# ScalarE copies the first step's columns in two parts, most of them before stage A ends

## The reference, cut to what matters

```python
xf = jnp.fft.rfft2(x, axes=(1, 2), norm='ortho').reshape(B, H, W // 2 + 1, 8, 96)
o1r = relu(xr @ w1[0] - xi @ w1[1] + b1[0])          # per block of 96 channels
o1i = relu(xi @ w1[0] + xr @ w1[1] + b1[1])
o2r = o1r @ w2[0] - o1i @ w2[1] + b2[0]
o2i = o1i @ w2[0] + o1r @ w2[1] + b2[1]
o = softshrink(stack([o2r, o2i]), 0.01)
out = jnp.fft.irfft2(complex(o), s=(H, W), axes=(1, 2), norm='ortho') + x
```

## Time and profile before

| | |
|---|---|
| median of 3 runs | 5809.21 us (5808.68 to 5814.81) |
| the profiled execution, its own time | 5797.72 us |
| its span in the trace | 5795.8 us |
| mean granted clock of TensorE | 0.986 of full |
| busy PE, ACT, DVE, POOL | 96%, 63%, 62%, 22% of the span |

### The profile page before, as it was taken

How to read it: one execution, slowest core, us unless ns; L and a number is a source line. 1 busy time by engine, 2 the same in 40 slices (tenths; PEclk the granted TensorE clock), 3 DMA queues, 4 the chain that set the end, 5 groups by cost and what they waited for, 6 DMA issues and landing times.

```text
span 5795.8 us, 116890 instructions
## 1 busy us (share of the span) xinstructions
PE 5579.8 (96%) x41056; PEld 5526.2 (95%) x41056; DVE 3599.6 (62%) x7158; ACT 3651.7 (63%) x8208; POOL 1264.6 (22%) x810
## 2 busy tenths in 40 slices
PE   8999999999999999999999999999999999999997
PEld 8999999999999999999999999999999999999997
DVE  5656656566566665666756667566665666656666
ACT  6656666566666666656676666665666666567564
POOL 2211222112222022220222202222012221122200
PEclk9999999999999999999999999999999999999999
DMA  3331233312333113332133331233312333113311
GB/s 98 91 92 32 61 92 91 92 34 59 92 91 92 45 47 92 91 92 57 40 88 91 92 80 34 70 91 92 86 36 62 91 92 90 46 48 91 92 45 44
DMA packets 1118349, 426.50 MB, mean 74 GB/s; under 512 B 1117472, under 2 KB 1117600, under 8 KB 1117728
## 3 DMA queue, kind: packets, MB, share of 16 engines
q1 hardware_dynamic: 1117728, 418.29, 28.7%
HBM read 216.89 MB, written 201.33 MB: 72 GB/s over the span
## 4 chain that ended last, share of the span: by engine, by line
PE 94%; issue 2%; DVE 1%; ACT 1%; DMA 0%; DVEq 0%; SPq 0%; ACTq 0%
PE psum L508 16%; PE psum L521 12%; PE psum L522 12%; PE psum L568 12%; PE psum L532 12%; PE psum L552 6%; PE psum L554 6%; PE psum L580 3%; PE psum L549 3%; PE psum L550 3%; PE psum L551 3%; PE psum L581 3%; PE psum L582 3%; DVE x L474 1%; ACT columns L317 0%
## 5 line engine op out<-in xcount | busy, mean ns | idle before, releaser
L293 POOL TENSOR_TENSOR doubled<-x 128x768 f32<-128x768 f32 x248 | 359.8, 1451 | 4206.6 <-DMA x<-x 4186.5
L444 DVE TENSOR_SCALAR relu<-psum,b1t 128x128 f32<-128x128 f32 x1056 | 370.1, 351 | 1364.0 <-ACT hidden_high L359 1361.6
L521 PE MATMUL psum<-w1t,columns 96*128 96x192 f32 x4160 | 1036.7, 331 | 66.7 <-ACT columns L317 66.7
L522 PE MATMUL psum<-w1t,columns 96*128 96x192 f32 x4160 | 1030.0, 330 | 0.0
L508 PEld LDWEIGHTS psum<-mats,x 128*96 128x96 f32 x8192 | 932.4, 168 | 90.0 <-issue 67.9
L508 PE MATMUL psum<-mats,x 128*96 128x128 f32 x8192 | 941.5, 279 | 79.1 <-issue 62.5
L353 ACT ACTIVATE mixed<-psum 128x384 f32<-128x384 f32 (+1 forms) x1056 | 512.8, 486 | 746.7 <-PE psum L522 740.9
L380 ACT ACTIVATE sums_high<-psum 128x512 fp32r<-128x512 f32 x768 | 459.4, 598 | 764.1 <-PE psum L568 764.1
L532 PE MATMUL psum<-mats,mixed 128*128 128x128 f32 x6272 | 874.8, 275 | 0.0
L532 PEld LDWEIGHTS psum<-mats,mixed 128*128 128x128 f32 x6272 | 842.8, 192 | 0.0
L521 PEld LDWEIGHTS psum<-w1t,columns 96*128 96x128 f32 x4160 | 755.4, 199 | 73.6 <-ACT columns L317 73.6
(11 more groups left out here) (62 smaller groups left out, 8421.9 us busy)
## 6 DMA issues: line engine op xcount, KB each, us to landing
x<-x SPq DMA_DIRECT2D x160, 768.0 KB, 7.1
out<-x SPq DMA_DIRECT2D x160, 768.0 KB, 8.2
x<-x SPq DMA_DIRECT2D x32, 1488.0 KB, 10.2
out<-x SPq DMA_DIRECT2D x32, 1488.0 KB, 10.6
x<-x SPq DMA_DIRECT2D x32, 816.0 KB, 5.0
out<-x SPq DMA_DIRECT2D x32, 816.0 KB, 4.5
w2t<-L_conv_w SPq DMA_DIRECT2D x128, 36.0 KB
w2t<-L_conv_w SPq DMA_DIRECT2D x128, 24.0 KB
```

What stands on the lines that cost most here:

```text
L521: pe.matmul(bank_b(s)[:, k], re, w1t[par][:, BLOCK:], start=True, stop=False)
L522: last = pe.matmul(bank_b(s)[:, k], im, w1t[par][:, :2 * BLOCK], start=False, stop=True)
```

## The change

`gather(0)` is taken apart. Stage A runs from both ends to the middle, so after 24 of its 32 groups the slots 0 to 47 and 80 to 127 are in `U`. Behind the eviction of group 24 ACT now waits for `u_zeroed` and for its own count of 24, and copies these 96 slots of column 0 in two instructions (48 slots each); behind the eviction of group 25 it copies those of column 64, in two more. At the end of stage A it copies the middle 32 slots of each column, in two instructions, and the last of these counts `gathered`. The other steps keep their one instruction. No instruction of PE, DVE, POOL or SP changes.

```diff
+EARLY = 24
+INNER = (EARLY // 2 * A_SLOTS, SIZE - EARLY // 2 * A_SLOTS)
 ...
             def gather(s):
                 dst, k = columns[s % 2], len(STEPS[s])
-                if s == 0:
-                    for r, j in enumerate((0, SIZE)):
-                        last = act.activation(dst[:, :, :, r], U[0:BLOCK, :, j:j + 2].rearrange("p s k -> p k s"), ACT.Copy)
-                else:
-                    ...
-                last.then_inc(gathered, 1)
+                j = 2 * STEPS[s][0]
+                act.activation(dst[:, 0:k], U[0:BLOCK, :, j:j + 2 * k].rearrange("p s (k r) -> p k s r", r=2),
+                               ACT.Copy).then_inc(gathered, 1)
+
+            def gather_first(r, lo, hi):
+                j = r * SIZE
+                return act.activation(columns[0][:, :, lo:hi, r], U[0:BLOCK, lo:hi, j:j + 2].rearrange("p s k -> p k s"), ACT.Copy)
 ...
                         last.then_inc(a_copied, 1)
-                    act.wait_ge(u_zeroed, n + 2)
+                        if i + 1 == EARLY:
+                            act.wait_ge(u_zeroed, n + 2)
+                            act.wait_ge(a_copied, n * NA + EARLY)
+                        if i + 1 - EARLY in range(2):
+                            r = i + 1 - EARLY
+                            gather_first(r, 0, INNER[0])
+                            gather_first(r, INNER[1], SIZE)
                     act.wait_ge(a_copied, n * NA + NA)
-                    gather(0)
+                    gather_first(0, *INNER)
+                    gather_first(1, *INNER).then_inc(gathered, 1)
                     gather(1)
```

More of the change, by code:

```diff
@@ L314, in gather @@
                 dst, k = columns[s % 2], len(STEPS[s])
-                if s == 0:
-                    for r, j in enumerate((0, SIZE)):
-                        last = act.activation(dst[:, :, :, r], U[0:BLOCK, :, j:j + 2].rearrange("p s k -> p k s"), ACT.Copy)
-                else:
-                    j = 2 * STEPS[s][0]
-                    last = act.activation(dst[:, 0:k], U[0:BLOCK, :, j:j + 2 * k].rearrange("p s (k r) -> p k s r", r=2),
-                                          ACT.Copy)
-                last.then_inc(gathered, 1)
+                j = 2 * STEPS[s][0]
[4 more added lines that the diff above has]
+                return act.activation(columns[0][:, :, lo:hi, r], U[0:BLOCK, lo:hi, j:j + 2].rearrange("p s k -> p k s"), ACT.Copy)
             with act.Fori(0, PAIRS) as m:
```

## The result

The changed kernel takes 5756.25 us (median of 5 runs, 5752.93 to 5766.13), the kernel before in the same sessions 5811.16 us. The ratio is 0.9905 with a 95% interval from 0.9891 to 0.992: faster by 0.95%, 55 us. The forecast was 5752, with a range from 5737 to 5776. The profiled execution of the changed kernel took 5760.14 us, its span is 5758.2 us.

A forecast was written before the change was run, and what follows sets the result against it. PE, busy 96% of the span, was taken as the bound. A shorter wait before B (23.4 us) and no clock falls behind it (34.3 us) gave 57.7 us off 5809.2, so 5751.5 us, range 5737 to 5776.

The forecast's parts named there:

- The bound and the path: PE, 96% busy, sets the end; the gap before B shrinks 0.73 us a unit, 23.4 us in all.
- The price of the copies: ACT's line 325: 188 ns fixed plus 1.89 per element, so 309 ns for 64 elements, 369 for 96.
- What hides the four early copies: Stage A: ACT's idle 0.28 us before each eviction hides their 1.19 us; lag gone before the last group; cost nothing.
- the earlier wait for `u_zeroed`: ACT waits 8 groups earlier in stage A; 5.8 us of margin in second units; cost nothing.
- The clock: Behind the gap before B: all 14 falls of PE's clock go at 1.35 us, worth 34.3 us.
- rival 2: End copies shorten less: gap 1.76 us, wait worth 10 us, half the clock's share gives 5782 us; chance 0.08.
- What can spread it: Pair starts: four pairs more or fewer at the dearer price, 8 us; stalls from POOL's fold, 1.3 us each.
- the stalls beside POOL: First steps: DVE's subtraction slows beside POOL's fold and PE stands; a few more units at 1.3 us each.
- the dearer stage A: Behind the clock's fall at a pair's start, stage A takes 31.02 us or 29.56; 8 of 15 paid the former.
- Rival 1: Behind the gap before B the clock falls as often as before; only 23.4 us won, 5785.8 us; chance 0.08.
- rival 4: ACT copies cost the same whatever their size; gap 2.24 us, slower at 5819 us; chance 0.03.
- Rival 3: Stalls beside POOL in pairs' first units: 12 more at 1.3 us take back 16 us, 5767 us; chance 0.05.

The follow-up runs named there:

- The long pair at the end: Changed kernel with its four early copies, but the pair at the end of stage A copies all 128 slots again: 5811.1 us, ratio 1.0004.
- the filler in the gap: Kernel before with five matmuls of 128x128, result unread, on PE between stage A and B: 5760.0 us, ratio 0.9914.
- the later POOL: Changed kernel, but POOL starts to fold an input only when DVE is through the running unit's third step: 5754.8 us, ratio 0.9907.
- the two fastest kernels: Changed kernel plus copies by column, more early copies, later fold, filler before E, and three fillers before B (5712.8 us) or before the last step's D (5711.1 us).

## Why the prediction was right

- *The bound and the path.* Right. PE stayed the bound (97% busy), and the whole 0.78 us came through to PE in each unit: gap -25.0 us against -23.4 forecast. The long pair at the end undid it.
- *The price of the copies.* Right: 312 and 371 ns against 309 and 369. The 0.833 ns per element of the Trainium skill (ScalarE: Activation LUTs, What ACT_TABLE_LOAD costs) would have made the copy of 64 elements 239 ns long; the trace has 312, and it decides. The reason that I gave for the 1.89 ns per element, that each is read from another place, was wrong in the main: read as neighbours the copy still took 657 ns of 672, and written side by side 539. The 0.05 us too much was the second wait, which I had left at the end of stage A in the sum, although the change moves it.
- *What hides the four early copies, and the earlier wait for `u_zeroed`.* Right: the lag is gone at the 29th group, and with early copies and a long pair the time was that of the kernel before (ratio 1.0004, 0.9993 to 1.0014).
- *The clock.* Right in the main: 14 falls before, none after, and the filler in the gap shows that this term does not need the shorter wait. But my reason was only that 1.35 us is next to gaps that never had a fall, and nothing I had told where between 1.26 and 2.08 us the falls begin; that 1.30 us was short enough was in part luck. At 1.78 us 10 falls of 14 are left, where rival 2 had given back half of the clock's share for 1.76. The price of 34.3 us also holds one stall of 1.26 us (in the stretch of 105.70) that is none of the clock's.
- *What can spread it.* Named, and it came on the bad side: the stalls beside POOL took some 6 us (8 units, where I had "a few more"; 5.9 us is what the later POOL gave back), three more pairs paid the dearer stage A, and the standstill at the pairs' starts was 4.4 us longer. My reason for more stalls, that the fallen clock hides them, is not borne out: the kernels with 10 to 16 falls and a gap of 1.78 to 2.02 us have 5 to 8 of them. The stretches miss their forecast by 8.4 us in all; what the other 2.5 are is open. The falls before stage E, 5.9 us in the profile, I had not foreseen: none of these gaps had a fall in the trace that I read. This is why the stretches and stages behind the gap gave 20.0 us in the profile and not 34.3.
- *The rivals.* Rival 1 is refuted by the profile after (no fall) and rivals 2 and 4 by the durations of the copies. Rival 3 holds as a part, with some 6 us in place of 16.

In the medians the sum was 57.7 forecast and 54.9 measured. In the profiled pair it was 57.7 and 37.6 (5740.0 us forecast for the profiled execution, 5760.1 measured; sum of the stretches 3280 and 3289.7, mean clock 0.991 and 0.989). So the close fit of the medians is in part luck: the profiled pair fell 20.1 us short of the sum by the losses above, and the medians lie 17.3 us further apart than the pair, whose execution of the kernel before was a fast one.

## What to carry to other kernels

Ask of every gap of the bounding engine not only how long it is but what clock stands behind it; here the stretches behind the gaps were worth as much as the gaps themselves (25.9 and 25.0 us), and a few matmuls that compute nothing got it without shortening the wait. When a change takes away one kind of gap, look at the small ones that are left. And price an unseen size of a copy by elements, with the fixed part taken from two sizes of a like copy and the price per element from a copy of its own layout: both unseen sizes came out within 1%.

## What the runs showed of the hardware that was not expected

- TensorE's clock fell behind 10 to 16 of 32 gaps of 1.78 to 2.08 us and behind none of 32 of 1.30 us, in each of four profiles; between the two nothing was run.
- It did not always fall behind longer standstills: in the two fastest kernels it fell behind 12 of 15 (2.96 to 3.47 us) and 14 of 15 (2.95 to 3.62 us), in the kernel with five fillers behind all 15 (3.00 to 3.52 us).
- The same two gaps of 0.80 and 0.71 us were followed by 0 to 4 or by 13 falls of 16 in different profiles.
- An ACT copy of 256 fp32 elements took 672 ns (read and written apart), 657 (neighbours read together), 539 (written side by side) and 434 (both).
- With nine or ten matmuls more in PE's loop the standstill at its start was shorter, about 3.3 us each in place of 4.1 to 4.5; with three more it was 4.3.
- DVE's subtraction of 128x128 took 1.84 us beside a POOL instruction that had started 0.12 us earlier; its median is 0.29.
- One execution took 14694 us in place of 5735, with PE busy for 99% of it and a granted clock given as 1.00.
